# A rounded copy of the GELU output written by ScalarE from PSUM instead of cast by VectorE

## The chip, the cores and the metric

The kernel runs on one core of one Trainium2 chip. The metric is the time of one execution in microseconds (us) of device time; runs are compared by their median. A core has TensorE (PE, matmuls; PEld is its weight load), VectorE (DVE), ScalarE (ACT), GpSimd (POOL) and SyncE (SP, which issues the DMAs here). The engines run on their own and wait for one another on semaphores.

## The reference, cut to what matters

Four blocks run one after the other on x of shape (4, 256, 256). Each is attention to a context and then an MLP. L0 and L2 have one attention, L1 and L3 two. All MLPs have this form (L1 and L3 with the exact GELU, L0 with an RMS norm):

```python
h = norm(x)                       # (4*256, 256)
h = gelu(h @ w1 + b1) @ w2 + b2   # w1 (256, 1024), w2 (1024, 256)
x = x + h
```

## The kernel before, in words

The matmuls of an MLP are done in a rounded format, fp32r. To keep the precision, each operand is split in two: a high part, which is the value rounded to fp32r, and a low part, the value minus the high part. A product is then three matmuls: high by high, low by high, high by low. For the hidden layer the parts are `hidH` and `hidL`; `hid` is the full GELU output, and `hidL` is written over it in place. All three lie in the large tiles that the trace calls arena and arena_r (two names of the same memory).

The four MLPs are called M0 to M3. An MLP works in B = 4 tiles of 256 rows, b = 0 to 3. One tile goes through these steps:

- DVE takes the statistics of the rows (L1458 or L1460 to L1462), POOL the power -1/2 (L486), and DVE writes the normalised rows `z` (L1467 or L1468).
- PE transposes z (`turn_m`, L614). ACT writes the transposed rows twice from PSUM, in full as `hT` and rounded as `hH` (`turned_m`, L1189). DVE subtracts them to `hL` (`mlp_split`, L1491).
- PE computes the 8 blocks f of the hidden layer in pairs, 6 matmuls a block (`up`, L631 to L633).
- ACT writes `hid` from PSUM (`gelus`, L1200), 128x256 for each f. It counts up `hid_ready`.
- DVE casts a pair of blocks, 128x512, to `hidH` (`hidden_high`, L1498) and counts up `hidH_ready`. POOL then writes `hidL` (L538) and counts up `hidL_ready`.
- PE computes the second matmul with hidH and hidL (`down`, L650 to L652), and DVE adds the result to x (L1561).

PE runs up(1), down(0), up(2), down(1), up(3), down(2), down(3), so that a tile's hidden parts have the whole of the next tile's `up` to become ready, except at the end.

There is no scheduler: each engine's order is written out by hand, and the first tile of an MLP is worked into the end of the attention before it. M1 and M3 follow a token attention. There PE does: up(0) blocks 0 to 3, turn_m(1), an output (L919), up(0) blocks 4 and 5, the transposes of the last probabilities (`turn_p`, L907), the last output (L919), up(0) blocks 6 and 7, and then up(1), which waits for hL of tile 1. ACT does the matching GELUs, and copies the last transposed probabilities to SBUF (`turned_p`, L1306) between the third and the fourth pair of GELUs. DVE casts a pair, adds an output to x (L1662), casts, adds, casts the last pair, and then makes hL of tile 1. M0 and M2 follow other attentions, with the last two casts of tile 0 ahead of hL of tile 1 in the same way. In M0, L730 are matmuls of that attention, L1167 and L1453 its last copies and additions; in M2, L1740 is the addition to x.

The POOL engine writes hidL of a tile in four instructions, and only then takes the power for the tile after the next (L486). From this come z of that tile, DVE's work behind it, and so hL of the tile between.

Of the kernel before, what the change touches and what calls it, by code (L numbers as in the profile page):

```python
# [28 lines left out]
B = 4  # L29
# [3 lines left out]
TILES = TOK // P  # L33
# [5 lines left out]
FT = F // P  # L39
# [69 lines left out]
def build(nc, t):  # L109
    ctx = ExitStack()  # L110
    with ctx:
# [3 lines left out]
        def sem(name):  # L115
            return ctx.enter_context(nc.semaphore(name))
# [94 lines left out]
        hid = arena[:, 0:4096].rearrange("p (k f n) -> p k f n", k=2, f=FT)  # L211
        hidL = arena_r[:, 0:4096].rearrange("p (k f n) -> p k f n", k=2, f=FT)
        hidH = arena_r[:, 5632:9728].rearrange("p (k f n) -> p k f n", k=2, f=FT)
# [91 lines left out]
        hs_ready = sem("hs_ready")  # L305
        w_step = sem("w_step")
        w_split = sem("w_split")
        hidH_ready = sem("hidH_ready")
        hidL_ready = sem("hidL_ready")
        f1_ps = sem("f1_ps")  # L310
        hid_ready = sem("hid_ready")
# [3 lines left out]
        def col(name, i=0, n=1):  # L315
            at = COLS[name][0] + i
            return cols[:, at:at + n]
# [5 lines left out]
        def up_slot(l, b, f):  # L323

            if l == 2 and b == 0:
                bank, half = ((2, 4, 5, 6)[f // 2], f % 2)
            else:
                bank, half = f // 2, f % 2
            return ps[:, bank, half * 256:(half + 1) * 256]
# [89 lines left out]
        def _(pool):  # L419
# [107 lines left out]
            def mlp_rows(l, name):  # L527
                for b in range(B):
                    if b + 2 < B:
                        power(f"M{l}", b + 2, 2)  # L530
                    for n in (2 * b, 2 * b + 1):
                        if l > 0:
                            pool.wait_ge(zm_ready, l * B + b + 1)
                        add_row(x, n, name)
                    for pair in range(FT // 2):
                        two = slice(2 * pair, 2 * pair + 2)
                        pool.wait_ge(hidH_ready, (l * B + b) * FT // 2 + pair + 1)
                        g.tensor_tensor(hidL[:, (b + 1) % 2, two, :], hid[:, (b + 1) % 2, two, :], hidH[:, b % 2, two, :].bitcast(F32),  # L538
                                        ALU.subtract).then_inc(hidL_ready, 1)
                    if l == 1 and b == 1:  # L540

                        pool.wait_ge(rows_done, rows_before("M1"))
                        g.memset(arena[:, 9728:14912], 0.0).then_inc(kc_step, 1)
                        pool.wait_ge(kc_step, 1)
                        g.memset(VC[0:C, :, :, 0, HD:VO], 1.0).then_inc(kc_clear, 1)
                        pool.wait_ge(kc_clear, 1)
                        g.memset(VC[C:P, :, :, 1, HD:VO], 1.0).then_inc(kc_clear, 1)
                        pool.wait_ge(kc_clear, 2)
# [555 lines left out]
        def _(act):  # L1104
            a_ = nc.scalar.activation
# [87 lines left out]
            def gelus(l, b, fs):  # L1193

                n = l * B + b
                _, _, bias, gelu = MLP[l]
                for f in fs:
                    if f % 2 == 0:
                        act.wait_ge(f1_ps, n * FT + f + 2)
                    a_(hid[:, (b + 1) % 2, f, :], up_slot(l, b, f), gelu, bias=col(bias, f)).then_inc(hid_ready, 1)  # L1200
                    if f == FT // 2 - 1 and 1 <= b < B - 1:
                        turned_m(l, b + 1)
# [10 lines left out]
            for i in range(N + 4):  # L1213
                step, b = i % 16, i // 16
# [166 lines left out]
        def _(dve):  # L1381
            v = nc.vector
# [108 lines left out]
                v.tensor_tensor(hL[:, b % 2, :, :], hT[:, b % 2, :, :], hH[:, b % 2, :, :].bitcast(F32), ALU.subtract)\  # L1491
                    .then_inc(hs_ready, 1)

            def hidden_high(l, b, pair):

                dve.wait_ge(hid_ready, (l * B + b) * FT + 2 * pair + 2)
                two = slice(2 * pair, 2 * pair + 2)
                v.tensor_copy(hidH[:, b % 2, two, :], hid[:, (b + 1) % 2, two, :]).then_inc(hidH_ready, 1)  # L1498

            N = TILES * PAIRS  # L1500
            for i in range(N + 3):
                step, b = i % 16, i // 16
# [21 lines left out]
                    mlp_z(0, (i - 56) // 2)  # L1524
                elif i == N:
                    mlp_split(0, 0)
            hidden_high(0, 0, 0)
            hidden_high(0, 0, 1)

            def weights(a, h):  # L1530

# [22 lines left out]
            def mlp(l):  # L1554
                base = l * B

                def add(b):
                    dve.wait_ge(f2_ps, base + b + 1)

                    dve.wait_ge(xb_ready, TILES * XB_AT[f"M{l}"] + 2 * b + 2)  # L1560
                    v.tensor_tensor(x[:, 2 * b:2 * b + 2, :], ps[:, 5:7, 0:D], x[:, 2 * b:2 * b + 2, :], ALU.add)\  # L1561
                        .then_inc(rows_done, 1)

                mlp_split(l, 1)
                for b in range(B):
                    if b == 0:
                        dve.wait_ge(rows_done, rows_before(f"M{l}"))
                    if b + 2 < B:
                        mlp_spread(l, b + 2)
                        mlp_z(l, b + 2)  # L1570
                    if b >= 1:
                        hidden_high(l, b, 0)
                        hidden_high(l, b, 1)
                        if b + 1 < B:
                            mlp_split(l, b + 1)
                        hidden_high(l, b, 2)
                        hidden_high(l, b, 3)
                        add(b - 1)
                if l == 1:
                    dve.wait_ge(zmT_ps, base + B)  # L1580
                    dve.wait_ge(rows_done, rows_before("M1") + B // 2 + 1)
                    first_z2()
                if l % 2 == 0:
                    weights(l, 0)
                    keys_rest(l, 0)
                add(B - 1)
# [35 lines left out]
            def tokens(a, seq):  # L1622
# [56 lines left out]
                    if g >= 2:  # L1679
                        add(g - 2)  # L1680
                if a % 2 == 1:
                    hidden_high(a, 0, 0)
                    hidden_high(a, 0, 1)
                    add(TILES - 2)
                    hidden_high(a, 0, 2)
                    add(TILES - 1)
                    hidden_high(a, 0, 3)
                else:
                    add(TILES - 2)
                    weights(a + 1, 0)  # L1690
                    keys_rest(a + 1, 0)
                    add(TILES - 1)

            def attend2(seq):
# [25 lines left out]
                for i in range(TILES + 3):  # L1720
# [26 lines left out]
                    if i == TILES - 3:  # L1747
                        dve.wait_ge(rows_done, rows_before("L2") + 2)
                        mlp_spread(2, 0)
                    elif i == TILES - 2:  # L1750
                        mlp_z(2, 0)
                        dve.wait_ge(rows_done, rows_before("L2") + 4)
                        mlp_spread(2, 1)
                    elif i == TILES - 1:
                        mlp_z(2, 1)
                    elif i == TILES + 1:
                        hidden_high(2, 0, 0)
                        hidden_high(2, 0, 1)
                hidden_high(2, 0, 2)
                hidden_high(2, 0, 3)  # L1760


            XB_AT = {"M0": 1, "T0": 2, "T1": 3, "M1": 4, "L2": 5, "M2": 6, "T2": 7, "T3": 8, "M3": 9}

            rows0(TILES - 2)
            rows0(TILES - 1)
            hidden_high(0, 0, 2)
            hidden_high(0, 0, 3)
            mlp(0)
            keys(0, 0)  # L1770
            tokens(0, 0)
# [124 lines left out]
```

## Time and profile before

| what | value |
|---|---|
| median of 3 runs | 1025.57 us (1023.36 to 1027.22) |
| the profiled execution, its own time | 1028.54 us |
| its span, first to last instruction | 1026.7 us |
| mean granted clock of TensorE in it | 0.971 |
| busy: PE, DVE, ACT, POOL | 930.8, 659.3, 489.1, 490.4 us |
| DMA: bytes, mean rate over the span | 52.48 MB, 51 GB/s |

The span is what the trace covers; the time of the execution has 1.84 us more around it. A matmul's duration overlaps that of the next, so PE's busy time says where PE had work, not how near its peak it is. What matters here is the idle time just before an instruction, and what ended it.

### The profile page before, as it was taken

Reading aid. Unit: us, or ns where it says so; the run is one execution under the profiler, and the core shown is the slowest. Engines: PE = TensorE matmul, PEld = TensorE weight load, DVE = VectorE, ACT = ScalarE, POOL = GpSimd, SP = SyncE. Lnnn points to the kernel's source line nnn. Section 1 sums busy time; section 2 is a strip of 40 time slices with the busy share of each in tenths; the row PEclk is TensorE's granted clock in tenths of the full one; section 3 lists DMA queues with packets and bytes.
Section 4 is the critical chain, followed back from the end, with each engine's and each line's share of the span. In section 5 each row is a group of like instructions: output and inputs, shape, how many; then the busy total and the mean of one; then the engine's idle time right before and its main releaser. Section 6 shows DMA issues by size and latency. Waiting matters only on the chain.

```text
span 1026.7 us, 16224 instructions
## 1 busy us (share of the span) xinstructions
PE 930.8 (91%) x5784; PEld 778.6 (76%) x5784; DVE 659.3 (64%) x1444; ACT 489.1 (48%) x1172; POOL 490.4 (48%) x509
## 2 busy tenths in 40 slices
PE   5899989889998999989889899899998989989898
PEld 3677877789894678846679688789985779856698
DVE  2566758463778847698645455363778847798552
ACT  3777767632673336733433343532663327632541
POOL 2645657365453324545448143084443325455373
PEclk7899999999999999999999998899999999999999
DMA  9000000000461004310000200020470004200000
GB/s 350 31 1 2 2 1 1 1 2 1 128 227 67 1 1 139 109 62 1 1 21 1 83 2 1 1 94 11 155 256 1 1 21 144 83 1 0 2 11 31
DMA packets 15026, 52.48 MB, mean 51 GB/s; under 512 B 1507, under 2 KB 4067, under 8 KB 13796
## 3 DMA queue, kind: packets, MB, share of 16 engines
q1 hardware_dynamic: 14948, 51.46, 14.5%
q8 instruction: 47, 0.77, 0.3%
q14 instruction: 31, 0.25, 0.1%
HBM read 50.41 MB, written 1.05 MB: 50 GB/s over the span
## 4 chain that ended last, share of the span: by engine, by line
PE 74%; DVE 14%; ACT 5%; issue 4%; POOL 3%; DMA 0%; SPq 0%; DVEq 0%; ACTq 0%
PE ps L895 8%; PE ps L919 7%; PE ps L822 5%; PE ps L824 5%; PE ps L862 5%; PE ps L851 4%; PE ps L730 4%; PE ps L631 3%; PE ps L633 3%; PE ps L632 3%; PE ps L717 3%; PE ps L650 3%; PE ps L651 3%; PE ps L652 3%; PE ps L706 2%
## 5 line engine op out<-in xcount | busy, mean ns | idle before, releaser
L895 PE MATMUL ps<-arena,hT 128*128 128x512 f32 x256 | 121.7, 620 | 19.5 <-ACT hT L1247 19.5
L919 PE MATMUL ps<-arena,pT_all 128*128 128x256 f32 x512 | 116.4, 380 | 6.1 <-ACT pT_all L1306 4.7
L494 POOL TENSOR_TENSOR arena<-arena,rinv 128x640 f32<-128x640 f32 x64 | 80.4, 1256 | 84.8 <-DVE rinv L1447 84.8
L519 POOL TENSOR_TENSOR prob<-prob,rinv 128x512 f32<-128x512 f32 x32 | 49.5, 1547 | 135.2 <-DVE rinv L1655 135.2
L486 POOL TENSOR_TENSOR rstd<-var,neg_half 128x1 f32<-128x1 f32 (+1 forms) x56 | 35.5, 633 | 158.7 <-DVE var L1462 158.7
L919 PEld LDWEIGHTS ps<-arena,pT_all 128*128 128x128 f32 x512 | 94.8, 190 | 19.4 <-ACT pT_all L1306 5.6
L895 PEld LDWEIGHTS ps<-arena,hT 128*128 128x128 f32 x256 | 49.2, 197 | 73.4 <-issue 49.0
L1200 ACT ACTIVATE arena<-ps,cols 128x256 f32<-128x256 f32 x128 | 53.4, 475 | 103.9 <-PE ps L633 103.9
L1313 ACT ACTIVATE prob<-prob 128x512 f32<-128x512 f32 x32 | 20.2, 630 | 163.0 <-DVE prob L1643 163.0
L538 POOL TENSOR_TENSOR arena_r<-arena,arena_r 128x512 fp32r<-128x512 f32 x64 | 87.4, 1387 | 13.5 <-DVE arena_r L1498 13.5
L631 PE MATMUL ps<-hH,w1H 128*128 128x256 f32 x256 | 77.6, 303 | 14.2 <-DVE hL L1491 8.2
L462 POOL TENSOR_TENSOR vacc<-vacc,vpart 128x256 f32<-128x256 f32 x60 | 44.1, 734 | 89.9 <-ACT vpart L1282 89.6
L1432 DVE TENSOR_REDUCE nb<-ps 128x2 f32<-128x640 f32 x64 | 52.6, 822 | 53.4 <-PE ps L706 52.6
L633 PE MATMUL ps<-hH,w1L 128*128 128x256 f32 x256 | 75.3, 294 | 0.0
L632 PE MATMUL ps<-hL,w1H 128*128 128x256 f32 x256 | 75.1, 293 | 0.0
L650 PE MATMUL ps<-w2H,arena_r 128*128 128x256 f32 x256 | 72.5, 283 | 1.6 <-DVE x L1561 1.6
L1157 ACT ACTIVATE arena<-ps,nb 128x320 f32<-128x320 f32 x128 | 66.3, 523 | 14.4 <-DVE nb L1432 11.7
L651 PE MATMUL ps<-w2L,arena_r 128*128 128x256 f32 x256 | 72.0, 281 | 0.0
L652 PE MATMUL ps<-w2H,arena_r 128*128 128x256 f32 x256 | 71.8, 280 | 0.0
L851 PE MATMUL ps<-HL,wq 128*128 128x256 f32 x384 | 67.0, 310 | 0.0
L453 POOL TENSOR_TENSOR u<-ring,lnb 128x256 f32<-128x256 f32 x64 | 66.6, 1040 | 0.0
L862 PE MATMUL ps<-ring,VT 128*128 128x256 f32 x256 | 65.9, 379 | 0.3 <-DVE x L1561 0.2
(164 smaller groups left out, 2441.1 us busy)
## 6 DMA issues: line engine op xcount, KB each, us to landing
ring<-in_heads_dram SPq DMA_DIRECT2D x64, 512.5 KB, 3.4
w<-in_w_dram SPq DMA_DIRECT2D x8, 1024.0 KB, 7.3
x<-in_x_dram SPq DMA_DIRECT2D x1, 1024.0 KB, 10.1
lnb<-in_lnb_dram SPq DMA_DIRECT2D x4, 256.0 KB, 9.0
ring<-in_wp_dram SPq DMA_DIRECT2D x1, 1024.0 KB, 5.3
out_dram<-x SPq DMA_DIRECT2D x4, 256.0 KB, 2.2
arena<-in_kinT_dram SPq DMA_DIRECT2D x1, 960.0 KB, 7.5
brow<-in_brow_dram SPq DMA_DIRECT2D x1, 768.0 KB, 11.4
```

The costliest lines, as they stand in the source:

```text
L494: g.tensor_tensor(w, w, rinv[:, n % 2, 0:2].unsqueeze(2).broadcast_to([P, 2, KEYS0]), ALU.mult)\
L538: g.tensor_tensor(hidL[:, (b + 1) % 2, two, :], hid[:, (b + 1) % 2, two, :], hidH[:, b % 2, two, :].bitcast(F32), ALU.subtract).then_inc(h ...
L631: mm(o, w1H[:, d, block], hH[:, k, d, :], start=(d == 0), stop=False)
L632: mm(o, w1H[:, d, block], hL[:, k, d, :], start=False, stop=False)
L633: last = mm(o, w1L[:, d, block], hH[:, k, d, :], start=False, stop=(d == 1))
L650: mm(o, hidH[:, k, f, at], w2H[:, f, :], start=(f == 0), stop=False)
L651: mm(o, hidH[:, k, f, at], w2L[:, f, :], start=False, stop=False)
L652: last = mm(o, hidL[:, 1 - k, f, at], w2H[:, f, :], start=False, stop=(f == FT - 1))
L851: last = mm(ps[:, 2 + k, d * B * C:(d + 1) * B * C], wq[:, k, c, d * P:(d + 1) * P], KT[:, k, e, :], start=(p == 0), stop=(p == 2))
L862: last = mm(ps[:, 4 + k, g * D:(g + 1) * D], VT[:, k, g * P:(g + 1) * P], ring[:, n % RING, WO:WO + D], start=True, stop=True)
L895: last = mm(ps[:, half, :], hT[:, k, d, 0:P], A[:, d, b // 2, cols_of, sl, :].rearrange("p r s k -> p r (s k)"), start=(d == 0), stop=(d = ...
L919: last = mm(ps[:, 6, 0:D], pT[:, k, c, :], VW[:, b, c, :], start=(c == 0), stop=(c == PAIRS - 1))
```

## The change

ACT now writes the GELU twice from the same PSUM block: first rounded to `hidH`, then in full to `hid`. DVE's casts (`hidden_high`) are gone with all their calls, and so is the semaphore `hidH_ready`. POOL's subtraction waits for `hid_ready` of ACT instead. The diff, cut to its core:

```diff
@@ POOL, mlp_rows
-                        pool.wait_ge(hidH_ready, (l * B + b) * FT // 2 + pair + 1)
+                        pool.wait_ge(hid_ready, (l * B + b) * FT + 2 * pair + 2)
@@ ACT, gelus
+                    a_(hidH[:, b % 2, f, :], up_slot(l, b, f), gelu, bias=col(bias, f))
                     a_(hid[:, (b + 1) % 2, f, :], up_slot(l, b, f), gelu, bias=col(bias, f)).then_inc(hid_ready, 1)
@@ DVE
-            def hidden_high(l, b, pair):
-
-                dve.wait_ge(hid_ready, (l * B + b) * FT + 2 * pair + 2)
-                two = slice(2 * pair, 2 * pair + 2)
-                v.tensor_copy(hidH[:, b % 2, two, :], hid[:, (b + 1) % 2, two, :]).then_inc(hidH_ready, 1)
@@ DVE, mlp
                     if b >= 1:
-                        hidden_high(l, b, 0)
-                        hidden_high(l, b, 1)
                         if b + 1 < B:
                             mlp_split(l, b + 1)
-                        hidden_high(l, b, 2)
-                        hidden_high(l, b, 3)
                         add(b - 1)
@@ DVE, tokens
                 if a % 2 == 1:
-                    hidden_high(a, 0, 0)
-                    hidden_high(a, 0, 1)
                     add(TILES - 2)
-                    hidden_high(a, 0, 2)
                     add(TILES - 1)
-                    hidden_high(a, 0, 3)
@@ DVE, attend2
-                    elif i == TILES + 1:
-                        hidden_high(2, 0, 0)
-                        hidden_high(2, 0, 1)
-                hidden_high(2, 0, 2)
-                hidden_high(2, 0, 3)
```

In M0 the four casts of tile 0 go likewise, two of them from just ahead of mlp(0).

On ACT, at the start of M1, this is the order before, from the four GELUs (L1200) that follow the table load: the copies hT and hH of tile 1, the third pair of GELUs, the copy of the last probabilities (L1306), and the fourth pair.

```order
L1189 ACTIVATE hH<-ps,cols 128x256 x2
L1200 ACTIVATE arena<-ps,cols 128x256 [waits f1_ps]
L1200 ACTIVATE arena<-ps,cols 128x256
L1306 ACTIVATE pT_all<-ps 128x512 [waits pT_ps]
L1306 ACTIVATE pT_all<-ps 128x512
L1200 ACTIVATE arena<-ps,cols 128x256 [waits f1_ps]
L1200 ACTIVATE arena<-ps,cols 128x256
```

The same place of the changed kernel, where L1199 is the rounded write and L1188 what was L1189:

```order
L1188 ACTIVATE hH<-ps,cols 128x256 x2
L1199 ACTIVATE arena_r<-ps,cols 128x256 [waits f1_ps]
L1200 ACTIVATE arena<-ps,cols 128x256
L1199 ACTIVATE arena_r<-ps,cols 128x256
L1200 ACTIVATE arena<-ps,cols 128x256
L1306 ACTIVATE pT_all<-ps 128x512 [waits pT_ps]
L1306 ACTIVATE pT_all<-ps 128x512
L1199 ACTIVATE arena_r<-ps,cols 128x256 [waits f1_ps]
L1200 ACTIVATE arena<-ps,cols 128x256
L1199 ACTIVATE arena_r<-ps,cols 128x256
L1200 ACTIVATE arena<-ps,cols 128x256
```

Four GELU writes instead of two now stand ahead of the copy of the probabilities, which the last output on PE waits for.

On DVE, at the same place of M1, the order before, from the last scaling of the probabilities (L1657) to hL of tile 1:

```order
L1657 TENSOR_TENSOR prob<-prob,rinv 128x512 [waits rinv_ready]
L1662 TENSOR_TENSOR x<-ps,x 128x256 [waits xb_ready,o_ps]
L1498 CAST arena_r<-arena 128x512 [waits hid_ready] x2
L1662 TENSOR_TENSOR x<-ps,x 128x256 [waits xb_ready,o_ps]
L1498 CAST arena_r<-arena 128x512 [waits hid_ready]
L1662 TENSOR_TENSOR x<-ps,x 128x256 [waits xb_ready,o_ps]
L1498 CAST arena_r<-arena 128x512 [waits hid_ready]
L1491 TENSOR_TENSOR hL<-hT,hH 128x512 [waits hm_ready]
L1460 BN_STATS stat<-x 128x6 [waits rows_done]
```

And now, where L1645 and L1650 are what was L1657 and L1662:

```order
L1645 TENSOR_TENSOR prob<-prob,rinv 128x512 [waits rinv_ready]
L1650 TENSOR_TENSOR x<-ps,x 128x256 [waits xb_ready,o_ps] x3
L1491 TENSOR_TENSOR hL<-hT,hH 128x512 [waits hm_ready]
L1460 BN_STATS stat<-x 128x6 [waits rows_done]
```

The subtraction hL now follows the third addition to x, without a wait for the last GELU of tile 0 between them. The third place is DVE in the middle of M1, from z of tile 3 on, before and now as one piece of the difference:

```order
 L1468 TENSOR_SCALAR z<-x,mv,rstd 128x256 [waits rstd_ready,zmT_ps]
 L1468 TENSOR_SCALAR z<-x,mv,rstd 128x256
-L1498 CAST arena_r<-arena 128x512 [waits hid_ready] x2
-L1491 TENSOR_TENSOR hL<-hT,hH 128x512 [waits hm_ready]
-L1498 CAST arena_r<-arena 128x512 [waits hid_ready] x2
-L1561 TENSOR_TENSOR x<-ps,x 128x512 [waits xb_ready,f2_ps]
```

With the minus rows the casts go; hL of tile 2 and the addition, in the changed kernel, follow z directly, in the same order.

## Rows read from the trace of the kernel before

**Rows 1.** The profile page: busy time by engine; chain that ended last, by engine.

```profile
PE 930.8 (91%) x5784; PEld 778.6 (76%) x5784; DVE 659.3 (64%) x1444; ACT 489.1 (48%) x1172; POOL 490.4 (48%) x509
...
PE 74%; DVE 14%; ACT 5%; issue 4%; POOL 3%; DMA 0%; SPq 0%; DVEq 0%; ACTq 0%
```

**Rows 2.** Timeline of PE: start us, us, operation, [idle before it <-releaser].

```profile
211.66 0.39 PE L631 MATMUL ps<-hH,w1H 128*128 128x256 f32 x1 [1.79 <-DVE hL L1491]
...
518.03 3.72 PE L919 MATMUL ps<-arena,pT_all 128*128 128x256 f32 x16 [1.18 <-ACT pT_all L1306]
...
525.17 0.39 PE L631 MATMUL ps<-hH,w1H 128*128 128x256 f32 x1 [1.99 <-DVE hL L1491]
...
529.01 0.66 PE L614 MATMUL ps<-ident,z 128*128 128x128 f32 x4 [0.71 <-DVE z L1468]
...
538.52 0.39 PE L631 MATMUL ps<-hH,w1H 128*128 128x256 f32 x1 [0.32 <-DVE hL L1491]
...
668.75 0.39 PE L631 MATMUL ps<-hH,w1H 128*128 128x256 f32 x1 [1.79 <-DVE hL L1491]
...
682.12 0.38 PE L631 MATMUL ps<-hH,w1H 128*128 128x256 f32 x1 [0.32 <-DVE hL L1491]
...
979.77 0.39 PE L631 MATMUL ps<-hH,w1H 128*128 128x256 f32 x1 [1.99 <-DVE hL L1491]
```

**Rows 3.** Chain of waits, M1's start: start us, us, what.

```profile
523.22 0.85 ACT arena L1200 x2
524.09 0.43 DVE arena_r L1498
524.51 0.60 DVE hL L1491
```

**Rows 4.** Timeline of ACT at four places.

```profile
207.35 0.47 ACT L1167 ACTIVATE arena<-ps,cols 128x256 f32<-128x256 f32 x1 [1.92 <-PE ps L730]
...
230.73 1.62 ACT L1200 ACTIVATE arena<-ps,cols 128x256 f32<-128x256 f32 x4
...
516.02 0.84 ACT L1200 ACTIVATE arena<-ps,cols 128x256 f32<-128x256 f32 x2 [2.66 <-PE ps L633]
516.89 1.08 ACT L1306 ACTIVATE pT_all<-ps 128x512 f32<-128x512 f32 x2
```

**Rows 5.** Instructions of three source lines: duration ns min/median/max, starts, shapes.

```profile
L1200 ACT ACTIVATE arena<-ps,cols x128: 465/473/512, 196.5 to 1011.4; 128x256 f32<-128x256 f32 x128
...
L1189 ACT ACTIVATE hT<-ps,cols x32: 553/565/573, 191.9 to 997.5; 128x256 f32<-128x256 f32 x32
L1189 ACT ACTIVATE hH<-ps,cols x32: 560/576/588, 192.8 to 998.4; 128x256 fp32r<-128x256 f32 x32
...
L538 POOL TENSOR_TENSOR arena_r<-arena,arena_r x64: 1279/1299/1753, 214.9 to 1013.1; 128x512 fp32r<-128x512 f32 x64
```

**Rows 6.** Timeline of DVE and then POOL in M1.

```profile
521.79 0.42 DVE L1662 TENSOR_TENSOR x<-ps,x 128x256 f32<-128x256 f32 x1 [4.47 <-PE ps L919]
...
534.62 1.48 DVE L1468 TENSOR_SCALAR z<-x,mv,rstd 128x256 f32<-128x256 f32 x2 [4.18 <-POOL rstd L486]
536.02 0.75 DVE L1498 CAST arena_r<-arena 128x512 fp32r<-128x512 f32 x2
536.69 1.78 DVE L1491 TENSOR_TENSOR hL<-hT,hH 128x512 fp32r<-128x512 f32 x1
...
536.51 3.10 POOL L538 TENSOR_TENSOR arena_r<-arena,arena_r 128x512 fp32r<-128x512 f32 x2 [0.57 <-DVE arena_r L1498]
```

**Rows 7.** Chain of waits, the starts of M0 and M2.

```profile
210.33 0.67 DVE arena_r L1498 x2
...
667.43 0.67 DVE arena_r L1498 x2
```

**Rows 8.** Windows: stretch, us, busy by engine (x), PEclk, DMA share, GB/s.

```profile
525.20:538.50 13.30, 12.29 (x100) 11.89 (x100) 7.96 (x20) 5.18 (x12) 11.26 (x12) 1.00 0.01 1
979.80:993.50 13.70, 13.70 (x103) 13.70 (x104) 8.38 (x20) 5.07 (x12) 11.65 (x12) 0.88 0.00 1
```

More of the change, by code:

```diff
@@ L307, in build @@
         w_split = sem("w_split")
-        hidH_ready = sem("hidH_ready")
         hidL_ready = sem("hidL_ready")
@@ L1526, in _ @@
                     mlp_split(0, 0)
-            hidden_high(0, 0, 0)
-            hidden_high(0, 0, 1)
             def weights(a, h):
@@ L1766, in _ @@
             rows0(TILES - 1)
-            hidden_high(0, 0, 2)
-            hidden_high(0, 0, 3)
             mlp(0)
```

## Prediction

> **What bounds the kernel now.** I read the page first. PE is busy 91% of the span, DVE 64%, ACT and POOL 48% each, and the chain that ended last lies on PE for 74% and on DVE for 14% [rows 1]. So DVE's casts are worth nothing as busy time; they count only where PE stands idle behind them. The next view is PE's timeline over the four MLPs, for the idle time that DVE ends [rows 2]. The reader is to see three kinds. Where up(1) starts, PE waits for hL of tile 1: 1.79 us in M0, 1.99 in M1, 1.79 in M2, 1.99 in M3. In M1 a wait of 0.71 follows before the transposes of z (L614), and one of 0.32 before up(2). M2 has that 0.32 too. In M0 and M3 neither of the later two appears. The chain through M1's start says what the 1.99 consists of: the last pair of GELUs 0.85, the cast 0.43, hL 0.60 [rows 3].
>
> **What ACT gains in work.** The change adds 128 GELU writes (4 MLPs, 4 tiles, 8 blocks), each of the form 128x256 from PSUM. Four in a row take 1.62 us and two take 0.84 [rows 4], so two more cost 0.78, or 0.39 each, and the total is 50 us on an engine that is busy 489 of 1026.7. Is a rounded write dearer? The trace has no GELU to fp32r. The nearest row is L1189, whose rounded writes have a median of 576 ns against 565 in full, from the same PSUM block [rows 5]. I take no difference; doubling a GELU's 473 ns is the far bound, and it is a rival below. A middle tile then costs ACT 16 x 0.39 and four copies for hT and hH, 4 x 0.57 at most, 8.5 us. PE's period for a tile is at least 538.52 - 525.17 = 13.35, less the waits of 0.71 and 0.32 in it, 12.3 [rows 2]. So within an MLP the added work is hidden by PE's matmuls. If that cover were gone, each of the 16 tiles would show the excess over 12.3.
>
> **Where it is not hidden.** In M1 the third pair of GELUs starts at 516.02, and the copy of the probabilities (L1306) starts right behind it, at 516.89 [rows 4]. PE waited 1.18 for this copy before its last output at 518.03 [rows 2]. Two more writes push the copy by 0.78, and with it the output, the third addition on DVE and the fourth pair. M3 has the same order. **Term: +0.78 in M1 and in M3**, to be set against what the starts gain. In M0 the GELUs of the third and fourth pair stand ahead of L1167, but that copy had waited 1.92 for PE [rows 4]; four more writes are 1.56, so 0.36 is left and the price is nothing. In M2 the last four GELUs come behind the attention's copies, and nothing on PE waits for them early.
>
> On this price a page of the Trainium skill can be set beside the rows. They show 0.39 us for each further write [rows 4]. ScalarE: Activation LUTs, "Rules for kernel authors", budgets about 0.3 us for an ACTIVATE with a bias operand and 0.83 ns an element, which makes an estimate of 0.51 for 256 elements. With it two writes cost 1.02 in place of 0.78, M1 and M3 gain 0.24 less each, and the sum below would be 0.5 smaller. The trace does not agree, 0.39, and the sum goes by the trace.
>
> **The starts of M1 and M3.** Before, hL stood behind ACT's last pair and a cast. Now it stands behind the third addition, which started at 521.79 and took 0.42 [rows 6]. With the push of 0.78 it ends at 522.99, and hL, 0.60 [rows 3], at 523.59. PE finished up(0) at 525.17 - 1.99 = 523.18, and with the push at 523.96 [rows 2]. So hL is ready 0.37 before PE asks, the wait is gone, and up(1) starts 1.99 - 0.78 = **1.21** earlier. What is late next is z of tile 2, whose chain starts at hL: hL ended at 525.11 [rows 3] and ends now at 523.59, 1.52 earlier. The transposes, which waited for z, start 1.52 earlier, so 0.40 of the 0.71 stays and M1's gain has grown to **1.52**.
>
> **The wait for up(2) in M1 and M2.** Before it stand, on DVE, z (1.48 us for two), two casts (0.75) and hL (1.78), and POOL's hidL writes beside them, 3.10 for two [rows 6]. Without the casts, hL can start 0.67 earlier (the two casts' share of the chain at the other starts) [rows 7]. An undisturbed hL takes 0.60 [rows 3], this one 1.78, because a POOL write of hidL was under way. POOL no longer waits for a cast (0.57 [rows 6]) and begins its write sooner, so hL may still meet it, for at most one write of 1.30 [rows 5]. Even then it ends 0.57 earlier than before, relative to z. The wait was 0.32, so I take it as gone: **0.32 in M1, 0.32 in M2**. The bounds are 0 and 0.32, for PE has nothing else to win there.
>
> **The starts of M0 and M2.** There hL stands behind the last addition of the attention and two casts, 0.67 in each [rows 7]. Nothing else is late: hT and hH are written long before. So up(1) starts **0.67** earlier in M0 and in M2, and 1.12 of each 1.79 stays. In M2 the later wait of 0.32 goes too.
>
> **The sum.** M0 0.67, M1 1.52 + 0.32 = 1.84, M2 0.67 + 0.32 = 0.99, M3 1.21: 4.71 us. One more thing depends on the clock. In M3 the granted clock was 0.88 from 979.80 to 993.50, against 1.00 in the same part of M1 [rows 8]; at the lower of its levels (1.2 in place of 2.4 GHz) it lost 0.12 x 13.70 = 1.64 us after the gap of 1.99. If the gap goes and this fall with it, M3 gains 1.64 and pays the wait for z that it did not show, 0.40: 1.2 more. M1 had the same gap and kept its clock, so I count one case in two, rounded down, **0.5**. In all 5.2 us. The profiled execution took 1028.54 (span 1026.7 and 1.84 around it), 2.97 above the median of 1025.57; it would go to 1023.3, and the median to **1020.4**, 0.5% less. The rest of the 50 us that DVE or ACT give or take (64 casts away, 128 writes added) is worth nothing, since PE waits for neither.
>
> **The rivals.**
> A. *The forecast*, gains of 4.5 to 7 us: 0.60.
> B. *The longer gap lowers the clock.* Before the last output PE stood 1.18 for the copy; now it stands 1.96. Gaps of 1.99 were followed by a fall in M3 and by none in M1 [rows 2, 8]. If the clock falls in both places, it costs 2 x 1.64 = 3.3, and the 0.5 is lost: a gain of 1.4, 1024.2. For it speaks M3, against it M1. The rule beside it is in TensorE: Matmul & The Clock Gate, "Part 1: The HAM clock gate": the clock follows recent activity as seen at moments that do not follow the kernel, so the same gap may be followed by a fall in one run and not in the next. Chance 0.20.
> C. *The gain is given back on hL.* hL loses to POOL more than once, or z takes longer since POOL runs without pauses; then PE keeps the 0.32 twice and the 0.31 of z that the sum took off, and the gain is 4.71 - 0.95 = 3.8, taken without the clock's 0.5: 1021.8. Nothing in the trace shows POOL passing DVE twice: hL met writes of 1.30 and took 1.78. Chance 0.13.
> D. *ScalarE becomes the bound, and it is slower.* If a rounded GELU from PSUM costs 2 x 0.473 = 0.95, a tile takes ACT 8 x 0.39 + 8 x 0.95 + 2.3 = 13.0, over PE's 12.3 by 0.7. In 12 middle tiles this is 8.4, and the push in M1 and M3 grows by 1.1 each; the starts give back some 2 of it: 1025.6 + 8, about 1034. It decides from (12.3 - 2.3 - 3.1) / 8 = 0.86 us a write on. The 576 against 565 ns of L1189 speak against it. Chance 0.04.
> E. *A larger gain*, because two falls of the clock (M0's and M3's starts) go with the gaps: 4.7 + 1.2 + 1.6 = 7.5 and more, 1018 or less. M0 keeps 1.12 of its gap. Chance 0.03.
>
> **Range and chances.** About what a measurement of this kernel can tell from no change is 0.5%, here 5.1 us. My forecast of 5.2 lies on that line. Of A a bit over half lies beyond it, and E whole; B, C and the rest of A are within it; D is slower, and a few cases of B with more falls of the clock. Faster 0.45, same 0.49, slower 0.06. The range goes from 1017.8 (a gain of 7.8, past E's) to 1024.6 (just past B's), which leaves out D and the tails of B.
>
> **What would show it in the profile of the changed kernel.** No CAST of 128x512 on DVE in the MLPs; 256 GELU writes at about 0.39 in a row. PE's wait before up(1) in M1 and M3 gone, 1.1 in M0 and M2. The idle time before the last output (L919) in M1 and M3 near 1.96. The wait before the transposes of z in M1 near 0.4, none before up(2). Wrong would be: a wait on DVE's hL still at M1's start (then hL was held by something other than the cast), a wait of PE on ACT inside a tile, or rounded writes that take longer than the others. A granted clock that differs from 0.971 by 0.005 moves the total by as much as the whole forecast, so PE's waits are to be compared before the totals.

## The result and the profile after

The changed kernel took a median of 1017.37 us in 7 runs, against 1025.57 in 7 runs of the kernel before. The ratio is 0.9912, with a 95% interval of 0.989 to 0.9934. It is faster by 0.9%, or some 8 to 9 us, where 5.2 us was forecast; the forecast range ended at 1017.8. One of the seven runs was disturbed (3245 us): it is in the median and not in the ratio, and the median of the other six is 1016.2.

The page of the changed kernel, with the rows that answer to [rows 1], and the rows of the rounded and the full GELU write:

```profile
PE 922.9 (91%) x5784; PEld 772.6 (76%) x5784; DVE 615.3 (61%) x1380; ACT 532.7 (52%) x1300; POOL 485.1 (48%) x509
...
PE 74%; DVE 14%; ACT 5%; issue 4%; POOL 2%; DMA 0%; SPq 0%; DVEq 0%; ACTq 0%; POOLq 0%
...
L1199 ACT ACTIVATE arena_r<-ps,cols 128x256 fp32r<-128x256 f32 x128 | 66.6, 520 | 61.3 <-PE ps L632 61.3
...
L1200 ACT ACTIVATE arena<-ps,cols 128x256 f32<-128x256 f32 x128 | 67.3, 526 | 0.0
```

PE's share of the chain is the same 74%. DVE is 44 us less busy and ACT 44 us more, and neither is what made the time: the gain lies in PE's waits. This is PE's timeline of the changed kernel at the places of [rows 2]; the number in brackets is the idle time before the row:

```profile
210.15 0.39 PE L630 MATMUL ps<-hH,w1H 128*128 128x256 f32 x1 [1.11 <-DVE hL L1491]
...
213.64 0.55 PE L613 MATMUL ps<-ident,z 128*128 128x128 f32 x3 [0.36 <-DVE z L1467]
...
514.09 0.48 PE L918 MATMUL ps<-arena,pT_all 128*128 128x256 f32 x1 [1.76 <-ACT pT_all L1306]
...
522.77 0.55 PE L613 MATMUL ps<-ident,z 128*128 128x128 f32 x3 [0.66 <-DVE z L1468]
...
659.54 0.39 PE L630 MATMUL ps<-hH,w1H 128*128 128x256 f32 x1 [1.11 <-DVE hL L1491]
...
663.37 0.55 PE L613 MATMUL ps<-ident,z 128*128 128x128 f32 x3 [0.70 <-DVE z L1468]
...
964.44 0.48 PE L918 MATMUL ps<-arena,pT_all 128*128 128x256 f32 x1 [1.76 <-ACT pT_all L1306]
...
973.13 0.55 PE L613 MATMUL ps<-ident,z 128*128 128x128 f32 x3 [0.67 <-DVE z L1468]
```

The starts of M1 and M3 have no wait for hL any more; no row of up(1) with idle time is left there. M0 and M2 kept 1.11 of 1.79. The waits of 0.32 before up(2) in M1 and M2 are gone. The gap before the last output (L918, which was L919) grew from 1.18 to 1.76. Before the transposes of z (L613) PE waits 0.36 in M0 and 0.66 to 0.70 in the others, in M3 too now. M2's 0.70 is not new: the kernel before has 0.71 there (at 672.60 in its first profile), which the prediction did not name; it stays, so it changes nothing in the sum.

The chain of waits of the changed kernel through the start of M1 (start us, us, what) shows what took the place of [rows 3]:

```profile
512.33 0.37 ACT arena_r L1199
512.69 0.36 ACT arena L1200
513.06 0.98 ACT pT_all L1306 x2
...
514.09 3.73 PE ps L918 x16
...
517.84 0.42 DVE x L1650
518.27 0.60 DVE hL L1491
...
521.24 1.49 DVE z L1468 x2
```

The four writes of the third pair now end just before the copy of the probabilities. On ACT's timeline they start at 511.49, 511.86, 512.22 and 512.57, 0.35 to 0.37 apart. Behind the output come the addition to x, hL and, by way of the statistics and the power, z. The last GELUs of tile 0 are off the chain.

### The profile page after: what moved, and what is told of

It is laid out like the page before. It is cut to its first block, busy times and chain, and to the rows that moved or that the text cites. A ratio compares the mean times of both kernels' runs of the same rounds, so it can differ in the third digit from the quotient of the medians.

```text
span 1015.6 us, 16288 instructions
## 1 busy us (share of the span) xinstructions
PE 922.9 (91%) x5784; PEld 772.6 (76%) x5784; DVE 615.3 (61%) x1380; ACT 532.7 (52%) x1300; POOL 485.1 (48%) x509
## 4 chain that ended last, share of the span: by engine, by line
PE 74%; DVE 14%; ACT 5%; issue 4%; POOL 2%; DMA 0%; SPq 0%; DVEq 0%; ACTq 0%; POOLq 0%
PE ps L918 7%; PE ps L894 7%; PE ps L821 5%; PE ps L823 5%; PE ps L861 5%; PE ps L850 4%; PE ps L729 4%; PE ps L649 3%; PE ps L650 3%; PE ps L651 3%; PE ps L716 3%; PE ps L630 3%; PE ps L631 3%; PE ps L632 3%; PE ps L705 2%
## 5 line engine op out<-in xcount | busy, mean ns | idle before, releaser
L918 PE MATMUL ps<-arena,pT_all 128*128 128x256 f32 x512 | 116.4, 380 | 7.3 <-ACT pT_all L1306 5.9
L918 PEld LDWEIGHTS ps<-arena,pT_all 128*128 128x128 f32 x512 | 94.8, 190 | 20.6 <-ACT pT_all L1306 6.8
L1199 ACT ACTIVATE arena_r<-ps,cols 128x256 fp32r<-128x256 f32 x128 | 66.6, 520 | 61.3 <-PE ps L632 61.3
L537 POOL TENSOR_TENSOR arena_r<-arena,arena_r 128x512 fp32r<-128x512 f32 x64 | 83.9, 1331 | 13.1 <-ACT arena L1200 13.1
L1200 ACT ACTIVATE arena<-ps,cols 128x256 f32<-128x256 f32 x128 | 67.3, 526 | 0.0
```

Of the source, the lines that this page charges most:

```text
L918: last = mm(ps[:, 6, 0:D], pT[:, k, c, :], VW[:, b, c, :], start=(c == 0), stop=(c == PAIRS - 1))
```

## The experiments

Each line below gives the median, the ratio to the kernel before on the same chip with its 95% interval, and the mean granted clock over the kernel's runs. The last is the mean over the runs of what each run's record gives. With it goes the **lost time**, span x (1 - clock): what TensorE's clock was short of its upper level. Over the 60 runs of the kernel before that went with the experiments the clock was 0.971 to 0.988, 0.9766 in the mean, so 23.9 us were lost, and the times had a mean of 1025.5. Within kernels, over 155 runs, a run was 0.59 us longer for each us more lost (a fit through each kernel's own mean; a third of the scatter, as variance, is left). The experiments ran on four chips, on which the kernel before had medians of 1023.6 to 1027.1; so the ratios compare more safely than the medians do.

| kernel | median us | ratio | 95% interval | mean clock |
|---|---|---|---|---|
| changed, first runs | 1017.37 | 0.9912 | 0.989 to 0.9934 | 0.9825 |
| e11_after (changed again) | 1017.59 | 0.9923 | 0.9902 to 0.9944 | 0.9807 |
| e13_before (before again) | 1025.92 | 0.9997 | 0.997 to 1.0025 | 0.9774 |
| e1_tile0 | 1017.87 | 0.9935 | 0.9909 to 0.9961 | 0.9820 |
| e2_tiles123 | 1021.14 | 0.9965 | 0.995 to 0.9981 | 0.9787 |
| e3_order | 1018.95 | 0.9939 | 0.9917 to 0.9962 | 0.9857 |
| e4_wait | 1023.09 | 0.9978 | 0.9962 to 0.9995 | 0.9775 |
| e5_copyfirst | 1012.94 | 0.9864 | 0.9843 to 0.9885 | 0.9835 |
| e6_best | 1015.39 | 0.9886 | 0.9857 to 0.9915 | 0.9787 |
| e7_longer | 1019.84 | 0.9933 | 0.9912 to 0.9954 | 0.9802 |
| e8_castslast | 1015.43 | 0.9891 | 0.9872 to 0.991 | 0.9837 |
| e9_stats | 1010.01 | 0.9852 | 0.9831 to 0.9873 | 0.9812 |
| e10_gap3 | 1015.22 | 0.9895 | 0.9877 to 0.9913 | 0.9837 |
| e12_gap1 | 1014.11 | 0.9901 | 0.9865 to 0.9937 | 0.9855 |

**Which tiles the gain comes from.** e1_tile0 changes tile 0 of each MLP alone, e2_tiles123 the other three alone. In e1:

```diff
 # ACT, gelus
+                    if b == 0:
+                        a_(hidH[:, b % 2, f, :], up_slot(l, b, f), gelu, bias=col(bias, f))
 # DVE, hidden_high
+                if b == 0:
+                    return
```

and e2 has `b > 0` in both places; POOL's waits follow.

> Only tile 0 of each MLP is changed: ScalarE writes both parts of its GELU, VectorE's casts of tile 0 are gone; tiles 1 to 3 keep the casts. Theory 1 (the gain lies at the starts, where hL of tile 1 and the statistics behind it stood behind casts and behind the last GELU of tile 0): nearly the whole gain, a median of 1017 to 1019 us, with only the wait of 0.3 before up(2) in M1 and M2 still there. Theory 2 (the casts of tiles 1 to 3 cost through POOL's ports and pauses): at most half of it, 1021 us or more.

> The reverse: tile 0 of each MLP is as before, with VectorE's casts; tiles 1 to 3 are changed. Theory 1: PE's waits of 1.8 and 2.0 us at the four starts stay, only the 0.3 before up(2) goes in two places, so 1024 to 1025.5 us. Theory 2: half of the gain or more, 1021 us or less.

Tile 0 alone gave 0.65%, the other tiles alone 0.35%, 1.0% together, where the whole was 0.88 and 0.77% in its two measurements. So most of the gain lies at the starts, as the first theory has it: e1 came out as expected. But e2, at 1021.14, gave more than that theory's one us and lies between the two expectations. Its profile has the 1.8 and 2.0 us before up(1) still there, and no wait before up(2) anywhere. How a wait before up(2) can be worth more than the forecast's 0.32 in two places is worked out below: it comes to 0.66 in M0 and 0.57 in each of the others, 2.4 us. Part of the 0.35% is also fewer falls of the clock, 0.9787 against 0.9766, worth 1.3.

**Is it hL alone, or the chain behind it?** e3_order keeps all casts and only makes hL of tile 1 ahead of the last casts of tile 0 (here for M1 and M3; M0 and M2 likewise):

```diff
                     add(TILES - 1)
+                    mlp_split(a, 1)
                     hidden_high(a, 0, 3)
```

> The kernel before with all casts, and one thing moved: hL of tile 1 is made ahead of the last casts of tile 0, in all four MLPs; the statistics of tile 2 stay behind those casts. If hL alone were what the starts wait for, PE's waits at M1's and M3's starts go without the later copy of the probabilities, and the time is 1017 to 1019. If the chain from the statistics of tile 2 to z counts as much (my reading), PE only waits later, before the transposes of z, for 1.5 to 2.5 us instead of 0.7, and the time is 1022 to 1025.

PE's timeline of e3_order before the transposes of z, in M1 (M3 has the same 2.34):

```profile
527.87 0.55 PE L614 MATMUL ps<-ident,z 128*128 128x128 f32 x3 [2.34 <-DVE z L1468]
```

The wait before up(1) is gone in M1 and M3, and 2.34 us stand before the transposes instead of 0.71: z was late next, as expected. The expectation of 1022 to 1025 failed nonetheless. The time was 1018.95, on the highest mean clock of all kernels, 0.9857. At 0.59 us for each us lost, its 9 us less of lost time than before are worth 5.5 us, and only 1 us is left for the waits.

**The wait put back.** e4_wait is the changed kernel with one line more on DVE:

```diff
+                dve.wait_ge(hid_ready, l * B * FT + FT)
                 mlp_split(l, 1)
```

> The changed kernel, with one wait added on VectorE: before hL of tile 1 it waits for the last GELU of tile 0, as the cast did. Theory 1: M1 and M3 lose what they won and more, since four GELU writes of 1.6 us end later than two and a cast of 1.3: a wait of about 2.3 us at each start, a median of 1023 to 1026. Theory 3 (the measured 8 us are for the most part a chance of where the granted clock falls, anywhere in the kernel): it stays near the changed kernel, 1017 to 1020.

```profile
522.21 0.39 PE L630 MATMUL ps<-hH,w1H 128*128 128x256 f32 x1 [2.38 <-DVE hL L1491]
```

That is PE's timeline of e4_wait at M1's start: 2.38 us of waiting, from this one line. M2 and M3 have 2.44 and 2.38. The median rose to 1023.09 and the mean clock fell to 0.9775 (12 runs each; the standard error of either mean is 0.0006). The theory that the gain was chance is refuted: the wait for the last GELU ahead of hL takes back 5 to 6 of the 8 to 9 us, with the clock that comes with it.

**The added writes ahead of the copy.** e5_copyfirst moves one copy on ACT in the changed kernel, and e7_longer adds one GELU write for each block of the third pair, to a tile that nothing reads:

```diff
 # e5_copyfirst
-                    gelus(a, 0, range(4, 6))
                 turned_p(TILES - 1)
                 if a % 2 == 1:
-                    gelus(a, 0, range(6, FT))
+                    gelus(a, 0, range(4, FT))
```

```diff
 # e7_longer
+                    if l % 2 == 1 and b == 0 and f in (4, 5):
+                        a_(spare[:, l // 2, f % 2, :], up_slot(l, b, f), gelu, bias=col(bias, f))
```

> The changed kernel with one thing moved on ScalarE: the copy of the last probabilities (L1306) stands ahead of the third pair of GELUs of tile 0 in M1 and M3, so the two added writes no longer push it. By the waits alone: PE's gap before the last output goes back from 1.76 to about 1.2 us in both places, 1.2 us in all, about 1015. By the clock theory (longer gaps of PE make the granted clock fall more often): the mean granted clock rises too, from 0.9825 to 0.985 or more, and the time is 1012.5 to 1014.5.

> The changed kernel, and the GELU of the third pair of tile 0 in M1 and M3 written once more by ScalarE, to a tile that nothing reads, so that the copy of the probabilities is pushed by 0.8 us again. By the waits alone: 1.5 us slower than the changed kernel, about 1018, at the same mean clock. By the clock theory: PE's gap of about 2.5 us lowers the granted clock more often, mean 0.979 or below, 1019 to 1022.

PE's timeline of e7_longer before the last output in M1:

```profile
514.87 0.48 PE L919 MATMUL ps<-arena,pT_all 128*128 128x256 f32 x1 [2.49 <-ACT pT_all L1309]
```

The gap is 2.49 us there (and in M3), against 1.76 in the changed kernel and 1.17 in e5. So a pair of writes ahead of the copy costs PE 0.73 where the copy stands right behind them. The first pair added cost 0.59: in e5, where no GELU is ahead of it, the copy starts 1.07 after the transposes of the probabilities, and in the kernel before it did so too, so there it had been waiting for PE and not for the GELUs. The times order as the gaps do: 1012.94, 1017.4, 1019.84. By the waits alone e5 should have won 1.2 us on the changed kernel and won about 4.5; e7 should have lost 1.5 and lost about 2.4. The mean clocks, 0.9835, 0.9816 and 0.9802, order the same way. Both clocks missed what the clock theory had expected (0.985 or more, 0.979 or below), and e5's 4 runs are few.

**The casts kept, only their place changed.** e8_castslast is the kernel before with hL of tile 1 and the statistics of tile 2 ahead of the last casts of tile 0, and nothing added on ACT (the moved calls of `mlp_split` are left out):

```diff
                         mlp_spread(l, b + 2)
+                        if b == 0:
+                            if l % 2 == 0:
+                                hidden_high(l, 0, 2)
+                            hidden_high(l, 0, 3)
                         mlp_z(l, b + 2)
```

> The kernel before with all of VectorE's casts and no added write on ScalarE, only the order changed: hL of tile 1 and the statistics of tile 2 stand ahead of the last casts of tile 0, which fill VectorE's wait for the power. If the place of the casts is what cost, and not their existence, PE has no wait before up(1) in M1 and M3, a short one before the transposes of z, and the time is that of the changed kernel or below, 1013.5 to 1017. If the casts also cost by their work in tiles 1 to 3 (waits of 0.3 before up(2)), 1 us more than that.

```profile
524.95 0.55 PE L614 MATMUL ps<-ident,z 128*128 128x128 f32 x3 [0.78 <-DVE z L1468]
...
534.46 0.39 PE L631 MATMUL ps<-hH,w1H 128*128 128x256 f32 x1 [0.32 <-DVE hL L1491]
```

PE's timeline of e8_castslast in M1 has 0.78 before the transposes of z and 0.32 before up(2), as expected, and no wait before up(1). At 1015.43 and a ratio of 0.9891 it is as good as the changed kernel (0.9912, 0.9923) or better. So what cost was where the casts stood, and not that DVE made them.

**More of the same order.** e6_best adds to e5 that hL of tile 1 is made ahead of the attention's last additions to x, in all four MLPs; e9_stats adds to e6 the statistics of tile 2 ahead of the last addition (here for M1 and M3; e5's change and the calls that go elsewhere are left out):

```diff
                     add(TILES - 2)
+                    mlp_split(a, 1)                                        # e6, e9
+                    dve.wait_ge(rows_done, rows_before(f"T{a}") + 6)       # e9
+                    mlp_spread(a, 2)                                       # e9
                     add(TILES - 1)
```

> The kernel of the copy moved first, and hL of tile 1 made ahead of the attention's last additions to x in all four MLPs. The waits of 1.1 us before up(1) in M0 and M2 should be gone. If z of tile 2 is late next, PE waits before its transposes for about that time more and nothing is won against the kernel it is made from; if fewer gaps at the starts also keep the clock up, 1 to 2 us: 1011 to 1013.

> The kernel with the copy moved first and hL moved first, and now the statistics of tile 2 also ahead of the attention's last addition to x, in all four MLPs, since z of tile 2 was late next (1.25 and 1.59 us in M0 and M2). PE's waits at the starts and before the transposes of z should all be near nothing; by the waits alone 1.5 to 2.5 us below the kernel with the copy moved first: 1010 to 1011.5. If the granted clock again falls more often, as it did with hL alone moved (mean 0.979), 1012 to 1014.

PE's timeline of e6_best before the transposes of z in M0 and M2, and then that of e9_stats in M0:

```profile
215.13 0.55 PE L613 MATMUL ps<-ident,z 128*128 128x128 f32 x3 [1.25 <-DVE z L1466]
...
662.39 0.55 PE L613 MATMUL ps<-ident,z 128*128 128x128 f32 x3 [1.59 <-DVE z L1467]
```

```profile
212.53 0.55 PE L613 MATMUL ps<-ident,z 128*128 128x128 f32 x3 [0.28 <-DVE z L1466]
```

In e6 the 1.11 before up(1) went in M0 and M2, and 0.9 of it came back before z (0.36 and 0.70 had stood there). Its mean clock was 0.9787. It is not clearly different from e5, and the 1011 to 1013 expected with a clock kept up was missed. In e9 z is early too; only 0.28 is left in M0 and nothing in the other three. It is the fastest version, 1010.01 us, 1.5% below the kernel before.

**One gap and the clock.** e10_gap3 is e5 with the wait of e4 in M3 only, e12_gap1 with that in M1 only:

```diff
+                if l == 3:        # e12: l == 1
+                    dve.wait_ge(hid_ready, l * B * FT + FT)
                 mlp_split(l, 1)
```

> The kernel with the copy moved first, and VectorE waits for the last GELU of tile 0 before hL of tile 1 in M3 only. M3 is the last of the kernel, so no stage behind it shifts. By the waits alone 1.5 to 1.8 us more than the kernel without it, about 1014.6, at the same mean clock, 0.983. By the clock theory this one gap of about 2.3 us lowers the clock in part of the runs: mean clock 0.9815 to 0.9825 and 1015 to 1016.5.

> As the kernel with the wait before hL of tile 1 in M3 only, but in M1 only. By the waits alone 1.8 us more than the kernel with the copy moved first (1012.9), 1014.7, at its mean clock of 0.983. If it is the gap in M1 that decides whether the clock falls in and after M1, the mean clock goes to 0.980 or below and the time to 1016 or more.

Windows of M1 and M3, from the first matmul of up(0) to the wait at the end, in e5_copyfirst, then of M3 in e10_gap3 (its M1 is that of e5, 59.15 at 1.00), then of both in e12_gap1. The columns are those of [rows 8]; the third from the end is the granted clock:

```profile
503.28:562.42 59.14, 55.73 (x436) 54.06 (x436) 18.34 (x45) 31.73 (x80) 39.37 (x38) 1.00 0.03 10
947.98:1001.88 53.90, 51.27 (x389) 49.80 (x389) 14.72 (x30) 31.84 (x80) 31.21 (x29) 0.97 0.03 11
```

```profile
947.28:1002.94 55.66, 51.32 (x388) 49.85 (x389) 14.24 (x30) 31.95 (x80) 31.22 (x29) 0.97 0.03 11
```

```profile
503.55:565.94 62.39, 57.27 (x436) 55.59 (x436) 18.44 (x45) 31.94 (x80) 39.50 (x38) 0.97 0.03 10
950.60:1003.01 52.41, 49.79 (x388) 48.32 (x388) 14.69 (x30) 31.73 (x80) 31.20 (x29) 1.00 0.03 11
```

Both gaps were 2.39 us. With the gap in M1, M1 took 62.39 instead of 59.14, and its clock was 0.97 where it had been 1.00. But M3, which is the same code in e12 and e5, took 52.41 in place of 53.90 and lost nothing: in e5 a fall stood at its beginning (0.60 from 947.98 to 952.20), in e12 none did. So this fall cost 1.49 us. With the gap in M3, M3 took 55.66. Its fall came after the gap; in e5, without the gap, there was one too, at M3's beginning. So the expectation that one gap lowers the mean clock failed for both, 0.9837 and 0.9855 against 0.9835. In these two profiles a fall came right behind the added gap, and one elsewhere did not come; one profile each doesn't show that the gap did both.

**Both kernels again.** e11_after is the changed kernel, e13_before the kernel before, both unchanged.

> The changed kernel again, unchanged, on the same chip as the two others, to have its times and granted clocks beside theirs and beside more runs of the kernel before. If fewer falls of the clock are part of the change's gain and not a chance of the first runs, its mean clock is again 0.981 to 0.984 against 0.975 to 0.978 of before, and the median 1015 to 1018.

> The kernel before, unchanged, for a second profile: the first one had a mean clock of 0.971, below the 0.976 to 0.977 of its runs since. If the extra gain is that before has falls of the clock in M1 and L2 which the changed kernel has not, this profile shows 1.5 to 2 us lost in M1 and 3 to 5 in L2 again, with about 5.8 instead of 7.8 before M0, where both kernels are the same. If the falls lie anywhere by chance, M1 or L2 show none.

e11 repeated the changed kernel's time; its mean clock, 0.9807, is just under the 0.981 that was expected and clear of before. Its four MLPs last as long as in the first profile within 0.1 us (M1 59.73 in both, M3 54.50 and 54.51). e13 is the run that settles most. As expected of it, M1 had a fall, the stretch between M1 and M2 lost time (0.96 over 565.19 to 642.67), and less was lost ahead of M0 (0.97 in place of 0.96 over the first 190 us). But the changed kernel has the same 0.96 between M1 and M2, so that stretch doesn't set the two kernels apart. PE's timeline of e13_before in M0 and then in M3; the rows around 974.34 are in full:

```profile
211.01 0.39 PE L631 MATMUL ps<-hH,w1H 128*128 128x256 f32 x1 [1.78 <-DVE hL L1491]
...
214.49 0.55 PE L614 MATMUL ps<-ident,z 128*128 128x128 f32 x3 [0.35 <-DVE z L1467]
...
224.37 0.39 PE L631 MATMUL ps<-hH,w1H 128*128 128x256 f32 x1 [0.68 <-DVE hL L1491]
...
972.07 0.28 PE L633 MATMUL ps<-hH,w1L 128*128 128x256 f32 x1
974.34 0.38 PE L631 MATMUL ps<-hH,w1H 128*128 128x256 f32 x1 [1.99 <-DVE hL L1491]
974.56 0.28 PE L632 MATMUL ps<-hL,w1H 128*128 128x256 f32 x1
...
978.19 0.55 PE L614 MATMUL ps<-ident,z 128*128 128x128 f32 x3 [0.71 <-DVE z L1468]
...
987.71 0.38 PE L631 MATMUL ps<-hH,w1H 128*128 128x256 f32 x1 [0.32 <-DVE hL L1491]
```

In this profile of the same kernel M0 has waits of 0.35 and 0.68 behind its 1.78, and M3 has 0.71 and 0.32 behind its 1.99. In the first profile neither MLP showed them [rows 2], because there the clock fell just after the gap, and with PE slower, z and hL came in time. Windows of 12 us from the start of up(1) in M0 to M3, in the first profile and then in e13_before, show it for all eight places:

```profile
211.66:223.66 12.00, 12.00 (x88) 12.00 (x89) 7.97 (x19) 5.14 (x12) 10.29 (x11) 0.86 0.01 1
525.17:537.17 12.00, 11.29 (x93) 11.08 (x94) 6.66 (x19) 5.18 (x12) 9.93 (x11) 1.00 0.01 1
668.75:680.75 12.00, 11.28 (x93) 11.08 (x94) 6.68 (x19) 5.18 (x12) 9.92 (x11) 1.00 0.54 196
979.77:991.77 12.00, 12.00 (x88) 12.00 (x89) 6.68 (x19) 5.07 (x12) 9.92 (x11) 0.86 0.00 0
```

```profile
211.01:223.01 12.00, 11.65 (x96) 11.45 (x97) 7.95 (x19) 5.19 (x12) 10.29 (x11) 1.00 0.00 1
520.78:532.78 12.00, 12.00 (x88) 12.00 (x89) 6.65 (x19) 5.14 (x12) 9.93 (x11) 0.86 0.01 3
661.03:673.03 12.00, 12.00 (x88) 12.00 (x89) 6.66 (x19) 5.08 (x12) 9.93 (x11) 0.86 0.53 196
974.34:986.34 12.00, 11.29 (x93) 11.09 (x94) 6.67 (x19) 5.19 (x12) 9.93 (x11) 1.00 0.00 0
```

Where the granted clock is 1.00, PE is idle for 0.35 to 0.72 us of the window, which is the wait before the transposes of z, and the wait before up(2) follows behind the window. Where the clock is 0.86, PE is busy for all 12.00 us, and its timeline has neither wait. The two profiles of one kernel are each other's opposite: M1 and M2 show the waits in the first, M0 and M3 in the second.

## Why the prediction was wrong

The windows of M0 to M3, first of e13_before, then of the changed kernel (first profile), and then M1 and M2 of the kernel before (first profile). M0, M1 and M3 begin with up(0), M2 with the output before it:

```profile
194.08:259.78 65.70, 60.48 (x480) 57.61 (x480) 29.46 (x56) 23.34 (x54) 33.44 (x33) 0.97 0.01 1
503.17:565.19 62.02, 57.29 (x437) 55.63 (x437) 30.31 (x61) 21.12 (x48) 41.63 (x38) 0.97 0.03 10
642.67:709.87 67.20, 63.61 (x478) 61.45 (x478) 29.37 (x62) 28.41 (x66) 33.16 (x33) 0.95 0.10 36
955.26:1012.03 56.77, 51.79 (x388) 49.93 (x388) 25.48 (x46) 21.17 (x48) 32.43 (x29) 0.97 0.03 10
```

```profile
193.88:258.27 64.39, 60.47 (x481) 57.61 (x481) 19.02 (x40) 34.12 (x86) 32.32 (x33) 0.97 0.01 1
503.02:562.75 59.73, 55.75 (x436) 54.08 (x436) 18.34 (x45) 31.74 (x80) 39.39 (x38) 1.00 0.03 10
640.24:707.79 67.55, 63.94 (x479) 61.41 (x479) 19.20 (x46) 39.42 (x98) 32.03 (x33) 0.95 0.10 36
951.88:1006.38 54.50, 51.28 (x389) 49.82 (x389) 14.71 (x30) 31.84 (x80) 31.23 (x29) 0.97 0.03 11
```

```profile
506.06:569.57 63.51, 57.75 (x436) 55.68 (x436) 30.13 (x61) 21.14 (x48) 41.22 (x38) 0.97 0.03 9
648.78:717.60 68.82, 64.19 (x479) 61.48 (x479) 29.36 (x62) 28.59 (x66) 33.13 (x33) 0.95 0.10 35
```

- **What bounds the kernel** was right: DVE's and ACT's busy time moved by 44 us each and meant nothing. The waits of PE named in [rows 2] are the ones that changed.
- **ACT's price** was right in its mechanism. The writes came 0.35 to 0.37 apart where 0.39 was taken, the rounded write costs no more than the full one (520 and 526 ns), and PE waited for ACT inside no tile. The push of the copy was 0.58, not 0.78, since the copy had itself been waiting for PE before.
- **M0: 0.67 forecast.** With one fall in each, just behind the first matmul of up(0), it is 65.70 in e13_before to 64.39, 1.31.
- **M1: 1.84 forecast.** The first profile took 63.51 with a fall just behind the first matmul of up(0), and M1 takes 59.73 now with none. A fall at the same place of M3 cost 1.49 (e5 against e12). Taking that for M1 too, an estimate, it is 62.02 to 59.73, 2.29.
- **M2: 0.99 forecast.** 68.82 to 67.55, 1.27, with 3.4 us lost in both, near the beginning of the window.
- **M3: 1.21 forecast.** With one fall in each, just behind the first matmul of up(0), 56.77 to 54.50, 2.27.

The four are 7.1 us, where the forecast had 4.7. **The step that failed first** is the reading of M0 and M3. The prediction took from one profile that "in M0 and M3 neither of the later two appears" and gave them terms of 0.67 and 1.21. Those waits are there whenever the clock does not fall just after the start of up(1), which e13 shows. The change takes away the wait before up(2) in both, and in M3 z comes earlier as it does in M1. By the forecast's own way of counting that is 0.68 more for M0 and 0.63 more for M3 (1.84 instead of 1.21), 1.3 in all. The prediction had the mechanism in its clock term, but there it valued it once, for M3, at one case in two, and it left M0 out.

**The second step** is the price of a wait. The forecast took each at its idle time, and put at nothing what it costs PE to run dry and start again. In the rows of e13_before the matmuls of a block start 0.12 apart, and across the wait of 1.99 it is 2.49 from 972.07 to 974.56 for two steps. So this wait costs 2.25, which is 0.26 more than the idle time. Across the 0.32 before up(2) of M3 it is 0.81 from 987.12 to 987.93, so that one costs 0.57. Five waits vanish whole (before up(1) in M1 and M3, before up(2) in M1, M2 and M3), worth 1.3 us more than was counted. The smaller push of the copy gives 0.2 more in M1 and in M3. Against both stands the wait for z, which is 0.66 there and not 0.40. With these, 4.7 + 1.3 + 1.3 + 0.4 - 0.5 is 7.2, and 7.1 was measured.

**The third step** is the size of the clock term, 0.5 us. The means of the runs differ by 8.4 us (1025.5 to 1017.1). With 7.1 at like falls, some 1.3 are left for falls that don't come; with the scatter of the runs this is 1.3 give or take about 1. The lost time itself went from 23.9 us (60 runs of before) to 18.7 (12 of the changed kernel, mean clock 0.9816), 3.1 us at 0.59 for each. The two ways of counting overlap and don't add, since a fall costs less where it hides a wait. M1 shows how much less: e13_before, with its fall just behind the start of up(1), took 62.02, no more than the 62.02 worked out for M1 with no fall at all. The forecast of 5.2 was short by some 3 us, of which a bit under half is the hidden waits of M0 and M3.

**Why the clock falls less often** is not settled. Shown is that the wait of e4, put into the changed kernel, lowers the mean clock from 0.9816 to 0.9775, and that kernels without the gaps before up(1) in M1 and M3 (e1, e3, e5, e8, e9) lie at 0.981 or above. But e6 and e7 have none of them either and lie at 0.9787 and 0.9802, single gaps in M1 or M3 lowered nothing, and e3, with gaps of 2.34 a little later in both, has the highest clock of all, 0.9857. Rival B, that the longer gap before the output makes a fall likely in both places, was not borne out: M1 had no fall, and M3's came ahead of that gap. The total of gaps does not predict the clock. The Trainium skill's page TensorE: Matmul & The Clock Gate, "Part 1: The HAM clock gate", has the clock follow recent activity by moments that are not tied to the kernel. The rows fit that: the same gap of 1.99 in M1 was followed by a fall in one profile of the kernel before and not in the other. No run here shows those moments, so it stays open which gap would bring a fall.

Rivals C and D didn't occur: the waits of 0.32 are gone in the changed kernel, and no write was dearer. Only C's longer wait before z is there, since up(1) starts earlier than was counted. Rival E, a larger gain because falls go with the gaps, is what came nearest. Its chance of 0.03 was too small, for the term on which it rested was one profile with a clock (0.971) at the bottom of the 60 runs.

## What to carry to other kernels

A wait that a profile doesn't show may be hidden by a slow stretch of the clock: compare the same stage in its repetitions (M0 with M2, M1 with M3) and take the one at full clock for what a change can win. A wait that vanishes whole is worth some 0.25 us more than its idle time here. Work off an engine is worth what stands behind it in that engine's queue. Here the order of three instructions on DVE won as much with all casts kept (e8) as the change did without them, and moving one copy on ACT ahead of the added writes (e5), and hL and the statistics ahead of the last addition (e6, e9), won almost as much again together: 1010.01 against 1017.4.

## What the runs showed of the hardware that was not expected

- Granted clock: stretches at 0.5 of it came at 6 to 13 places in a profile. The same kernel before had between 0.971 and 0.988 in 60 runs, and times of 1019.3 to 1029.3. A gap of 2.39 us on PE was followed by one in M1 (e12) and in M3 (e10), while a stretch elsewhere did not come.
- A fall of the clock just behind a wait can cost nothing: M1 of the kernel before took 62.02 us with a fall just behind the start of up(1) in e13_before, as much as is estimated above for M1 without one, and 63.51 with one at its beginning in the first profile.
- A wait costs PE about 0.26 us more than the idle time that a profile shows before the row: 2.25 for 1.99, and 0.57 for 0.32 (e13_before).
- A GELU from PSUM to a rounded tile, 128x256, has a mean of 520 ns in a queue of such writes and starts 0.35 to 0.37 us after the one ahead of it, the same as the full write (526 ns). Its duration is not its price: in the kernel before, with half as many in a row, the same write had a mean of 475 ns, and four of them took 1.62 us [rows 4], 0.37 for each after the first.
